# Layer 1 of a two-layer graph network: target logits from on-chip bf16 pieces and a compared one-hot, in place of four small loads and four transposes per group

## The reference

```
# layer 0: softmax per feature over the edges of a target
msg = h[src] + edge_attr ; s = msg * beta
e = exp(s - segment_max(s, dst)[dst])
agg = segment_sum(msg * e / segment_sum(e, dst)[dst], dst)
x = x + agg @ H + bias + h
# layer 1: graph attention, 4 heads of 32
Wx = (h @ W.T).reshape(n, 4, 32)
e = leaky_relu(Wx[src] . a[:32] + Wx[dst] . a[32:], 0.2)      # one logit per edge and head
ex = exp(e - segment_max(e, dst)[dst])
x = x + elu(segment_sum(ex * Wx[src], dst) / segment_sum(ex, dst))
```

## Time and profile before

| what | value |
|---|---|
| time, median of 3 runs | 2266.79 us (2266.45 to 2268.63) |
| profiled execution, first to last instruction | 3375.9 us |
| busy in the profiled execution | PE 2454.8, DVE 2003.4, POOL 1656.1, ACT 1356.4 us |
| packets moved by the DMA queues | 318,698, of these 169,938 under 512 bytes |
| first gather of layer 0 / last | 34.5 / 1614.2 us |
| first gather of layer 1 / last | 1726.1 / 3310.1 us |

### The profile page before, as it was taken

The page is one execution under the profiler, slowest core; times in us unless marked ns, Lnnn a source line. Parts: engine busy times, 40 slices in busy tenths (PEclk is TensorE's granted clock), DMA queues, the critical chain, the costliest instruction groups (busy, mean ns, idle before and its releaser), DMA issues.

```text
span 3375.9 us, 63284 instructions
## 1 busy us (share of the span) xinstructions
PE 2454.8 (73%) x15346; PEld 2205.4 (65%) x15347; DVE 2003.4 (59%) x3854; ACT 1356.4 (40%) x3494; POOL 1656.1 (49%) x1741
## 2 busy tenths in 40 slices
PE   2777777767676776767756878777778777787777
PEld 1666666656565665656646777777767776787776
DVE  5655655556565565566744565566555555665556
ACT  2444444444344444444622333333333333333335
POOL 5444554545445445454534545544445444555443
PEclk8888888888888888888866767777777777777678
DMA  5332332323323323333022222222112112222111
GB/s 157 91 89 82 88 87 87 88 80 88 84 83 86 87 81 88 86 89 91 8 66 39 40 38 40 40 38 38 38 37 40 37 36 38 40 41 39 36 36 50
DMA packets 318698, 213.54 MB, mean 63 GB/s; under 512 B 169938, under 2 KB 279074, under 8 KB 318642
## 3 DMA queue, kind: packets, MB, share of 16 engines
q0 software_dynamic: 53184, 112.31, 13.4%
q1 hardware_dynamic: 264608, 100.15, 11.5%
q10 hardware_dynamic: 850, 0.43, 0.0%
HBM read 200.69 MB, written 10.29 MB: 62 GB/s over the span
## 4 chain that ended last, share of the span: by engine, by line
another core or an unknown queue 34%; PE 26%; issue 14%; ACT 12%; DVE 7%; ACTq 3%; POOL 2%; DMA 1%; SPq 0%; DVEq 0%; POOLq 0%
PE sums L1309 14%; ACT acc L773 4%; DVE sums L1063 2%; PE sums L1325 2%; ACTq L755 2%; ACT carried L765 2%; PE sums L1329 2%; DVE seg_max L1068 2%; ACT banks L804 2%; PE banks L1407 2%; PE banks L1416 1%; PE banks L1398 1%; PE banks L1425 1%; PE banks L1318 1%
## 5 line engine op out<-in xcount | busy, mean ns | idle before, releaser
L677 POOL DMA_INDIRECT msg<-wx_dram,meta_g x831 | 792.9, 954 | 831.5 <-DVE prod L1215 420.7
L640 POOL DMA_INDIRECT ring_h<-h_dram,meta_g x831 | 792.7, 954 | 789.4 <-ACT banks L804 468.8
L1309 PE MATMUL sums<-onehot,prod 128*128 128x128 f32 x3296 | 818.9, 338 | 301.5 <-ACT acc L773 268.8
L1309 PEld LDWEIGHTS sums<-onehot,prod 128*128 128x128 f32 x3296 | 659.2, 248 | 338.8 <-issue 337.6
L1309 PE MATMUL sums<-onehot,wgt 128*128 128x128 f32 x3296 | 792.6, 329 | 19.3 <-issue 19.3
L1309 PEld LDWEIGHTS sums<-onehot,wgt 128*128 128x128 f32 x3296 | 655.4, 246 | 20.2 <-issue 20.1
L765 ACT ACTIVATE carried<-acc,scale 128x2 f32 x414 | 122.7, 296 | 965.9 <-remote 578.0
L1325 PE MATMUL sums<-msg,beta_ident 128*128 128x512 f32 x416 | 268.8, 733 | 299.6 <-ACT sums L790 217.4
L773 ACT ACTIVATE acc<-sums 128x1022 f32 x410 | 419.7, 1024 | 0.0
L1098 DVE TENSOR_TENSOR prod<-sums,msg 128x512 f32<-128x512 f32 x208 | 143.0, 688 | 460.5 <-ACT sums L790 330.2
L1329 PEld LDWEIGHTS sums<-neg_ident,seg_max 128*128 128x128 f32 x1664 | 268.4, 229 | 128.0 <-issue 122.8
(11 more groups left out here) (177 smaller groups left out, 3059.4 us busy)
## 6 DMA issues: line engine op xcount, KB each, us to landing
msg<-in_edge_attr SPq DMA_DIRECT2D x207, 256.0 KB
flags<-flag_dram SPq DMA_DIRECT2D x52, 512.2 KB
window<-wx_dram SPq DMA_DIRECT2D x832, 2.0 KB
ring_h<-h_dram,meta_g POOLq DMA_INDIRECT x831
msg<-wx_dram,meta_g POOLq DMA_INDIRECT x831
wx_dram<-msg SPq DMA_DIRECT2D x13, 272.0 KB, 2.1
nodes<-in_x SPq DMA_DIRECT2D x6, 512.0 KB, 7.1
h_dram<-acc SPq DMA_DIRECT2D x12, 256.0 KB
```

The costliest lines, as they stand in the source:

```text
L640: pool.indirect_dma_start(hg[0:n, s % HRING, b, :], None, h_dram, bass.IndirectOffsetOnAxis(ap=meta_g[0:n, s, b:b + 1], axis=0)).then_inc( ...
L677: pool.indirect_dma_start(msg[0:n, s, b, :], None, wx_dram, bass.IndirectOffsetOnAxis(ap=meta_g[0:n, s, b:b + 1], axis=0)).then_inc(L1["ga ...
L1309: ins = pe.matmul(where[:, j, bass.ds(off, P)], what[:, slot, b, :], onehot[:, s, b, :], start=(b == 0), stop=(b == GB - 1), skip_group_ch ...
```

## The change

After the change, layer 1 makes no window loads. While `wx_dram` is made, POOL splits each batch's target logits into three bf16 numbers that add up to the fp32 one (`split_logits`: a cast, a subtraction, a cast, a subtraction, a cast), PE turns them (`turn_logits`, four matmuls), and DVE copies them from PSUM into `node_logit`, 12 rows by all nodes in SBUF (`keep_logits`). Per group PE then takes four windows out of `node_logit` by four small matmuls at computed addresses (`windows1`), ACT copies them (128x48 in place of 128x512), and PE multiplies as before, but with three bf16 pieces per block (12 matmuls for 4).

The transposed one-hots no longer come from PE. The edges' places are stored once as a bf16 row in `key_dram`; SP broadcasts it to all partitions, four groups at a time (512 KB), and DVE compares it with the partition's number (`one_hotT1`).

```diff
+            sp.wait_ge(key_flat, 1)
+            sp.dma_start(key_dram[0:ct * P * P].rearrange("(t c e) -> c t e", c=P, e=P), key_b[:, 0:ct, :]
+                         ).then_inc(keys_stored, 16)
...
             def load1(g, s, use):
-                if s % HALF == 0 and later(g, 1):
+                if s % HALF:
+                    return
+                if later(g, 1):
                     load_lists(g, s, use, L1)
...
                 if later(g, RING):
-                    sp.wait_ge(L1["targets"], g - (RING - 1))
-                first = sp.value_load(blk_row[0:1, 1, bass.ds(g * GB, 1)], min_val=0, max_val=N - 1)
-                offset = offsets(sp, g)
-                for b in range(GB):
-                    sp.dma_start(window[:, s, b, :], wx_dram[bass.ds(first + offset[b], P), D + H:TW]).then_inc(L1["windowed"][s], 16)
+                    sp.wait_ge(L1["onehotsT"], g - (RING - HALF))
+                    apart(sp)
+                run = key_dram[bass.ds(g * GE, HALF * GE)].rearrange("(a e) -> a e", a=1)
+                sp.dma_start(key_rows[:, s // HALF, :], run.to_broadcast([P, HALF * GE])).then_inc(L1["keyed"][s // HALF], 16)
...
+            def split_logits(b, u, use):
+                t = 1 if isinstance(b, int) and b == NBAT - 1 else GB
+                logits = msg[:, u, 0:t, D + H:TW]
+                rest = piece_rest[:, 0:t, :]
+                pool.wait_ge(mid_wx, b + 1)
...
+                for i in range(PIECES):
+                    piece = pieces[:, u % 2, 0:t, i * H:(i + 1) * H]
+                    left = logits if i == 0 else rest
+                    ins = pool.tensor_copy(piece, left)
+                    if i < PIECES - 1:
+                        ins.then_inc(piece_made, 1)
+                        pool.wait_ge(piece_made, step + 2 * i + 1)
+                        pool.tensor_tensor(rest, left, piece, ALU.subtract).then_inc(piece_made, 1)
+                        pool.wait_ge(piece_made, step + 2 * i + 2)
+                ins.then_inc(pieces_made, 1)
...
-                act.activation(onehotT[:, s % 2, :], bank[0][:, :], ACT.Copy).then_inc(L1["spread"], 1)
+                act.activation(window[:, s % 2, :, :].rearrange("p b k -> p (b k)"), window_psum, ACT.Copy
+                               ).then_inc(L1["spread"], 1)
...
+            dve.wait_ge(keys_made, 1)
+            dve.tensor_copy(key_b[:, :, :], dst_f[:, :, :]).then_inc(key_flat, 1)
...
-            sweep(dve, NBAT, WXB, [(1, hT1), (3, wx1)])
+            def keep_logits(b, u, use):
+                dve.wait_ge(pieces_psum, b + 1)
...
+                    dve.tensor_copy(node_logit[:, bass.ds(b * GE, GE)].rearrange("h (p t) -> h t p", t=GB),
+                                    sums[0:PIECES * H, u % 2, 0, :].rearrange("h (t p) -> h t p", t=GB)
+                                    ).then_inc(pieces_kept, 1)
+
+            sweep(dve, NBAT, WXB, [(1, hT1), (5, keep_logits), (3, wx1)])
...
+            def one_hotT1(g, s, use):
+                dve.wait_ge(L1["keyed"][s // HALF], 16 * (use + 1))
+                if later(g, 2):
+                    dve.wait_ge(L1["targets"], g - 1)
+                lo = s % HALF * GE
+                dve.tensor_scalar(onehotT[:, s % 2, :], key_rows[:, s // HALF, lo:lo + GE], place[:, 0:1], None, ALU.is_equal
+                                  ).then_inc(L1["onehotsT"], 1)
...
-            sweep_edges(dve, [(6, products1), (3, logits1), (5, shift1), (4, maxima1), (0, one_hot1)], until=NG + 2)
+            sweep_edges(dve, [(6, products1), (3, logits1), (5, shift1), (4, maxima1), (1, one_hotT1), (0, one_hot1)], until=NG + 2)
...
-            def onehotT1(g, s, use):
-                pe.wait_ge(L1["onehots"], g + 1)
+            def windows1(g, s, use):
+                node = pe.value_load(blk_row[0:1, 1, bass.ds(g * GB, 1)], min_val=0, max_val=N - 1)
+                offset = offsets(pe, g)
                 if later(g, 1):
                     pe.wait_ge(L1["spread"], g)
                 for b in range(GB):
-                    ins = pe.transpose(bank[0][:, b * P:(b + 1) * P], onehot[:, s, b, :], ident[:, :])
-                ins.then_inc(L1["onehotsT"], 1)
+                    ins = pe.matmul(window_psum[:, b * PIECES * H:(b + 1) * PIECES * H],
+                                    node_logit[:, bass.ds(node + offset[b], P)], ident_b[0:PIECES * H, 0:PIECES * H],
+                                    start=True, stop=True)
+                ins.then_inc(L1["windowed"], 1)
...
                 for b in range(GB):
-                    ins = pe.matmul(bank[1][:, b * H:(b + 1) * H], onehotT[:, s % 2, b * P:(b + 1) * P], window[:, s, b, :],
-                                    start=True, stop=True)
+                    for i in range(PIECES):
+                        ins = pe.matmul(target_psum[:, b * H:(b + 1) * H], onehotT[:, s % 2, b * P:(b + 1) * P],
+                                        window[:, s % 2, b, i * H:(i + 1) * H], start=(i == 0), stop=(i == PIECES - 1))
```

More of the change, by code:

```diff
@@ L99, in gnn_kernel @@
     HRING = 4
+    PIECES = 3
     assert NT % GB == 1 and (NBAT - 1) % WXB == 0 and WGT == WXB and NG % RING == 0
@@ L128, in gnn_kernel @@
         junk = sb("junk", [1, 1])
+        place_i = sb("place_i", [P, 1], I32)
+        place = sb("place", [P, 1])
         zero_row = sb("zero_row", [1, WIN], BF16)
@@ L167, in gnn_kernel @@
         aggT = ring_h[:, 2:4, :]
+        node_logit = shared[0:PIECES * H, :, :].rearrange("p r e -> p (r e)").bitcast(BF16)[:, 0:N + WIN]
         FIN = 4
-        pos = sb("pos", [P, 2, GE])
-        elu_e = sb("elu_e", [P, 2, GE])
-        fin = sb("fin", [P, 2, GE])
+        pos, elu_e, fin = (shared[:, i:i + 2, :] for i in range(HRING, HRING + 6, 2))
         def over(buffer):
@@ L185, in gnn_kernel @@
         flags = sb("flags", [P, 2, HALF * GE + 1], BF16)
-        window = sb("window", [P, RING, GB, H])
+        ident_b = sb("ident_b", [P, P], BF16)
+        window = sb("window", [P, 2, GB, PIECES * H], BF16)
+        key_b = sb("key_b", [P, CT, P], BF16)
+        pieces = sb("pieces", [P, 2, GB, PIECES * H], BF16)
+        piece_rest = sb("piece_rest", [P, GB, H])
         seg_max = sb("seg_max", [P, 2, GE])
@@ L1174, in wx1 @@
                     dve.wait_ge(wx_stored[u], 16 * use)
+                    apart(dve)
+                    dve.wait_ge(pieces_made, b - (WXB - 1))
                 if not (isinstance(b, int) and b == NBAT - 1):
@@ L1387, in layer_in, with turn_logits @@
                 ins.then_inc(mid_wx_psum, 1)
-            sweep(pe, NBAT, 2, [(1, turn_h), (2, layer_in)])
-            pe.wait_ge(mid_wx, NBAT)
-            def onehotT1(g, s, use):
-                pe.wait_ge(L1["onehots"], g + 1)
+            def turn_logits(b, u, use):
+                pe.wait_ge(pieces_made, b + 1)
+                if later(b, 2):
+                    pe.wait_ge(pieces_kept, b - 1)
+                for t in range(1 if isinstance(b, int) and b == NBAT - 1 else GB):
+                    ins = pe.matmul(sums[0:PIECES * H, u, 0, t * P:(t + 1) * P], pieces[:, u, t, :], ident_b[:, :],
+                                    start=True, stop=True)
+                ins.then_inc(pieces_psum, 1)
+            sweep(pe, NBAT, 2, [(1, turn_h), (5, turn_logits), (2, layer_in)])
+            pe.wait_ge(mid_wx, NBAT)
+            pe.wait_ge(pieces_kept, NBAT)
+            pe.wait_ge(pads_made, 1)
+            def windows1(g, s, use):
+                node = pe.value_load(blk_row[0:1, 1, bass.ds(g * GB, 1)], min_val=0, max_val=N - 1)
+                offset = offsets(pe, g)
                 if later(g, 1):
@@ L1397, in onehotT1 @@
                 for b in range(GB):
[L1398 to L1399 removed]
+                    ins = pe.matmul(window_psum[:, b * PIECES * H:(b + 1) * PIECES * H],
+                                    node_logit[:, bass.ds(node + offset[b], P)], ident_b[0:PIECES * H, 0:PIECES * H],
+                                    start=True, stop=True)
+                ins.then_inc(L1["windowed"], 1)
             def targets1(g, s, use):
                 pe.wait_ge(L1["spread"], g + 1)
[L1403 removed]
+                pe.wait_ge(L1["onehotsT"], g + 1)
                 if later(g, 1):
```

67 lines of the change are left out of this document (44 added, 23 removed).

## The result

The changed kernel takes 2660.51 us (2658.42 to 2664.47, 4 runs) against 2267.22 (2266.45 to 2268.63), a ratio of 1.1739, 95% interval 1.1725 to 1.1754: 393 us, 17%, slower. The prediction said 2276, at most 2302. Single executions that fell far from the rest, such as one of the kernel before that took 7464 us at a granted clock of 0.25, are left out of every ratio in this text.

A forecast was written before the change was run, and what follows sets the result against it. The prediction took POOL's gathers, 5.00 us a group, to pace both layers before and after. It added 5 us for the sweep and 4 for compares beside POOL to 2266.8, giving 2276, with a range of 2257 to 2302.

The forecast's parts named there:

- What bounds the kernel before: Both layers: POOL's gathers, 1.25 us apart and four per group, pace the kernel at 5.00 us a group.
- the sum of 2263: Kernel before: start, both layers' gathers at 1.25 us, the stretch between layers and the end add up to 2263 us.
- The loads and transposes that go: Layer 1, SP and PE: removed loads (3.55 us) and transposes (0.60) lie beside POOL's 5.00, new window matmuls fit: 0.
- The clock: Rival, PE in layer 1: waiting more, it falls to 1.2 GHz and paces; each tenth there costs 63 us; chance 0.05.
- The compare on DVE: Layer 1, DVE: one compare per group, 0.43 us (0.22 to 0.78), makes a step 4.9, under POOL's 5.00: 0.
- The compare beside POOL: Layer 1: DVE's compares slow gathers they overlap, 4 us in all; bounds 0 and 60.
- The rival "Faster": Layer 1: POOL's 29.9 us wait for `meta_g` goes with the window loads, or lighter PE gains; under 2262, chance 0.16.
- The sweep: Between the layers: `keep_logits` makes DVE's step 1.97 us against ACT's 1.59, over eleven steps; 5 us, bounds 0 and 6.1.
- The sum: Whole kernel: sweep 5 plus compare beside POOL 4 make 9 us, 2276, 0.4% slower.
- The range: Whole kernel: 2257 to 2302 us, leaving out about 1 in 10 below and 1 in 10 above.

The follow-up runs named there:

- fixed_windows_2: Changed kernel with fixed columns for the four window matmuls, so two register loads and their arithmetic go (target logits wrong): 2279.83 us, ratio 1.0055.
- compare_loaded: Changed kernel with windows loaded by SP as before, one-hots compared in fp32 on DVE, and no windows1 on PE: 2465.16 us, ratio 1.0862.
- compare_loaded_turns: compare_loaded with the four transposes put back on PE as work nobody reads: 2296.86 us, ratio 1.0140.
- turns_kept_2: Changed kernel with the four transposes of before kept on PE, their result unread: 2622.99 us, ratio 1.1561.
- one_load: Changed kernel without the second register load and its arithmetic in windows1; all four windows start at the first node (three blocks wrong): 2280.22 us, ratio 1.0063.
- lean_cheap_keep_2: Whole change with one load of four registers for the window starts and turned pieces written in node order, on a 2267 chip: 2275.60 us, ratio 1.0044.
- old_loop_dead_windows: old_loop with windows1 added on PE ahead of the transposes, its result overwritten: 2617.09 us, ratio 1.1546.
- old_loop: Changed kernel's setup and sweep with the layer-1 loop of before, on 3380 chips only: ratios 1.0052, 1.0043 and 1.0041 in three sets.
- lean_cheap_keep: Same kernel as lean_cheap_keep_2, run on a 3380 chip: ratio 1.0484.

## Why the prediction was wrong

**What bounds the kernel before: right, as far as the runs show.** POOL's gathers at 5.0 a group in both layers; there is no trace of the kernel before on a 2267 chip, but the changed kernel's layer 0 and fixed_windows_2's layer 1 (1184.1 to 2229.1, 1045.0) show that pace undisturbed, and the sum of 2263 rests on it. The reason given for the 3375.9 us was wrong (they come with the chip, not with the recording), and harmless only because rates were taken from unhindered stretches.

**The step that failed** is in "The loads and transposes that go": "The four window matmuls have 12 columns; with two register loads they fill at most the 0.60 that the transposes leave." It priced array time. The sequencer's stretch grew from 0.8 to 3.2 us per group, and all that it hands to the array meanwhile is four matmuls of 12 columns. Shown: taking it out (2280), halving it (2280) or shortening it with nothing left out (2276) removes the loss, and adding it to the old loop (2617) brings it.

**The clock, given 0.05.** The rival's mechanism was right and its chance too small; its cause was half told: less work on PE does it (compare_loaded), but in the changed kernel the long register stretch stands beside it. "The time before fits 5.0 us throughout" is no argument about a kernel with less work and a longer gap. Its price of 3 us a group was too high: 7.07 - 5.03 = 2.0. That the level matters by itself is shown by compare_loaded against compare_loaded_turns. How the changed kernel's 380 us (393 less the 13 that stay in fixed_windows_2) divide is only estimated, since it has no step wholly at the high level: by turns_kept_2's 5.63 against 5.03, some 0.6 x 208 = 125 us are the stretch as such, and the rest, some 255, the low level.

How the two combine, argued from the table of steps: where the high-level step is under 5.0 (4.72 to 4.75 in fixed_windows_2, one_load and lean_cheap_keep_2), PE makes up after a low step and POOL paces; where it is over 5.0 (5.63 in turns_kept_2), it never does. compare_loaded is between: 4.87 at the high level, 6.80 at the low one, 1.0 more than fixed_windows_2's 5.76, and it can stay low for long. Why PE leaves the low level after a few steps in one kernel and after up to 27 in the other, and hardly at all in old_loop_dead_windows (180 low steps of 183), stays open.

**The compare on DVE: right.** It took 0.33 us (0.43 taken, 0.22 to 0.78 the bounds), and its cover held. In compare_loaded, with an fp32 result, it took 0.47. By the Trainium skill (VectorE: DVE Perf Modes, The perf-mode tier table) bf16 on both sides is the faster tier; the two rows agree.

**The compare beside POOL: predicted 4 us, not told apart.** fixed_windows_2's layer 1 took 1045.0 us for its gathers, its layer 0 1043.0, and 830 steps of 1.25 are 1037.5: all that comes on top of the bare pace in layer 1 is 7.5 us, where the prediction had 6 before the change and 10 after. The compare's part of it no run tells: old_loop, whose loop is without it, ran on 3380 chips only. The rule that VectorE can shut GpSimd out for a whole instruction (the Trainium skill, SBUF — State Buffer, Who interferes with whom) shows no such loss here: 0.33 us per group would be 69.

**The rival "Faster", given 0.16: its stall was not there.** POOL's 29.9 us of waiting for `meta_g` came from a 3380 chip, and old_loop has 31.1 on one. old_loop_dead_windows, compare_loaded and compare_loaded_turns keep the window loads in the same line with the lists, and their traces, from 2267 chips, show no wait of POOL for `meta_g` in layer 1. So there was nothing to win.

**The sweep: predicted 5, measured 9.** The first hT copy to the first gather, from the line of that copy, before and after:

```profile
L1169 DVE COPY hT<-banks x13: 281/692/693, 1699.2 to 1719.0; 128x512 f32<-128x512 f32 x12, 128x128 f32<-128x128 f32 x1
```

```profile
L1204 DVE COPY turn_rows<-banks x13: 269/669/692, 1147.2 to 1173.6; 128x512 f32<-128x512 f32 x12, 128x128 f32<-128x128 f32 x1
```

1726.1 - 1699.2 = 26.9 before, 1183.0 - 1147.2 = 35.8 after. The kind of chip does not matter to it: old_loop, with the same sweep, has 35.8 too on a 3380 chip (1697.1 to 1732.9). The step, on DVE's timeline of the changed kernel:

```profile
1157.24 1.29 DVE L1223 CAST shared<-sums 12x512 bf16<-12x512 f32 x1
1158.34 0.32 DVE L1213 COPY msg<-sums 128x136 f32<-128x136 f32 x1
1158.58 0.55 DVE L1215 COPY msg<-banks 128x408 f32<-128x408 f32 x1
1159.07 0.67 DVE L1204 COPY turn_rows<-banks 128x512 f32<-128x512 f32 x1
1159.66 1.29 DVE L1223 CAST shared<-sums 12x512 bf16<-12x512 f32 x1
```

It is 2.42 us, not 1.97, and eleven steps of 2.42 - 1.59 are the 9: `keep_logits` takes 1.29, where 0.61 was taken and 0.78 was the upper bound. It writes bf16 with a stride of four; lean_cheap_keep_2, without the stride, has 0.67 on that line, and 32.1 us from first copy to first gather (1147.7 to 1179.8).

**The sum.** What does not concern PE came to 13 us (fixed_windows_2, one_load) where 9 was predicted: 9 of it the sweep, and some 4 that have no certain place; lean_cheap_keep_2 has the same 4 (9 less a sweep of 32.1 - 26.9 = 5.2).

**The range** ended at 2302 since every price in it was array or engine time; the one path that could lead far above it, the clock, was written off with 0.05.

## What to carry to other kernels

When a stage moves to an engine, count the register loads, address arithmetic and checks that its sequencer must do in a row, as time in which the engine is handed nothing, and compare that with what the array still has in its queue when they start; array time is not the price. Where PE's step at the 1.2 GHz level would be over the pace, work taken from PE can cost more than it gives: ask what the step is at both levels. An address table laid out so that one load brings all registers of a step is the cheap form.

## What the runs showed that was not expected

- Four unread transposes per group made a kernel 168 us faster (2465 to 2297).
- PE stayed at the 1.2 GHz level through work without a gap (70.00 of 70.00 us busy at 0.50 in compare_loaded, by a profile that models the ends of matmuls). The Trainium skill (TensorE: Matmul & The Clock Gate, What's actually happening) has a busy array back at full rate; here the measurement decides.
- A load of four registers takes 0.33 us, of one 0.31.
- A DVE copy of 12x512 from PSUM to bf16 takes 1.29 us with a stride of four in the write and 0.67 without.
- The same kernel takes 2267 us on one chip and 3380 on another, and a variant at 1.004 on the first stands at 1.048 on the second (lean_cheap_keep).
